# A pair mask added by GpSimd, or as the bias of ScalarE's copies of attention scores (one core)

## What is computed

```python
Q = (x @ Wq.T).reshape(b, s, h, hd)      # 16 heads of 16
K = (x @ Wk.T).reshape(b, s, h, hd)
V = (x @ Wv.T).reshape(b, s, h, hd)
scores = jnp.einsum('bshd,bstd->bsht', Q, K) / math.sqrt(hd)
attn = jax.nn.softmax(scores, axis=-1)
out = jnp.einsum('bsht,bstd->bshd', attn, V).reshape(b, s, dm)
return out @ Wfc.T
```

## Time and profile before

| | |
|---|---|
| median of three runs | 1049.65 us |
| lowest, highest | 1046.6, 1050.26 us |
| the profiled execution, first to last instruction (span) | 1045.7 us |
| mean granted PE clock over the span | 0.969 |
| PE busy | 959.2 us (92%) |
| DVE busy | 690.6 us (66%) |
| ACT busy | 496.8 us (48%) |
| POOL busy | 377.1 us (36%) |
| DMA: mean, small packets | 130 GB/s; 122142 of 133025 packets under 2 KB |

### The profile page before, as it was taken

How to read it: one execution, slowest core, us unless ns; L and a number is a source line. 1 busy time by engine, 2 the same in 40 slices (tenths; PEclk the granted TensorE clock), 3 DMA queues, 4 the chain that set the end, 5 groups by cost and what they waited for, 6 DMA issues and landing times. The chain is left out here.

```text
span 1045.7 us, 30362 instructions
## 1 busy us (share of the span) xinstructions
PE 959.2 (92%) x11177; PEld 823.6 (79%) x11178; DVE 690.6 (66%) x1747; ACT 496.8 (48%) x1343; POOL 377.1 (36%) x330
## 2 busy tenths in 40 slices
PE   6899999889999999999987999999767888999996
PEld 3466666879999999999965778888666878899995
DVE  3478877855777777777412688889985776344442
ACT  3556665404454554554446777777552440322221
POOL 0134335521223223222213455555561101455552
PEclk9999999999999999999998899999868999999998
DMA  9885581294232222221055657766421620444441
GB/s 338 216 331 122 126 269 41 97 386 115 85 102 79 87 97 85 89 92 71 8 107 92 115 124 150 154 134 128 99 68 57 266 108 22 151 134 140 134 136 35
DMA packets 133025, 135.59 MB, mean 130 GB/s; under 512 B 73884, under 2 KB 122142, under 8 KB 130740
## 3 DMA queue, kind: packets, MB, share of 16 engines
q1 hardware_dynamic: 121684, 90.80, 31.5%
q0 software_dynamic: 11232, 43.27, 13.0%
HBM read 96.21 MB, written 44.77 MB: 135 GB/s over the span
## 5 line engine op out<-in xcount | busy, mean ns | idle before, releaser
L1151 PE MATMUL psall<-rows 128*128 128x128 f32 x1872 | 224.8, 277 | 1.6 <-issue 1.1
L1151 PEld LDWEIGHTS psall<-rows 128*128 128x128 f32 x1872 | 219.6, 194 | 3.1 <-issue 1.3
L1114 POOL DMA_INDIRECT x<-ffn_rows,tok_i x78 | 82.6, 1059 | 171.8 <-DVE tok_i L999 69.9
L1165 PE MATMUL psall<-whi,rows 128*128 x624 | 141.0, 379 | 0.0
L1244 DVE COPY rows<-wlo 128x2048 f32 (+2 forms) x78 | 74.5, 955 | 95.8 <-PE psall L1151 85.2
L1165 PEld LDWEIGHTS psall<-whi,rows 128*128 128x128 f32 x624 | 115.7, 190 | 14.1
L1119 POOL DMA_INDIRECT attn_rows<-rows,tok_i x39 | 41.7, 1070 | 183.9 <-DVE rows L1276 183.9
L1504 DVE STREAM_TRANSPOSE whi<-whi 32x512 f32<-32x512 f32 x128 | 89.7, 701 | 9.1 <-POOL whi L1467 7.7
L1584 ACT ACTIVATE whi<-psall 32x512 f32<-32x512 f32 x128 | 75.3, 588 | 30.8 <-PE psall L1713 27.3
L280 PE MATMUL psall<-cst 128*128 128x128 f32 x714 | 88.4, 280 | 0.5 <-PEq L1387 0.5
L1306 ACT ACTIVATE rows<-psall,vs 128x128 f32<-128x128 f32 x312 | 85.0, 383 | 4.4 <-PE psall L1151 2.1
(11 more groups left out here) (250 smaller groups left out, 1731.3 us busy)
## 6 DMA issues: line engine op xcount, KB each, us to landing
ffn_rows<-mod_rows SPq DMA_DIRECT2D x2, 4096.0 KB
wlo<-in_W SPq DMA_DIRECT2D x2, 4096.0 KB, 17.5
whi<-in_w SPq DMA_DIRECT2D x5, 1024.0 KB
whi<-mod_rows SPq DMA_DIRECT2D x4, 1024.0 KB, 15.0
ffn_rows<-rows SPq DMA_DIRECT2D x8, 512.0 KB
ffn_rows<-x SPq DMA_DIRECT2D x8, 512.0 KB
wlo<-attn_rows SPq DMA_DIRECT2D x32, 128.0 KB, 3.4
v_turn<-wlo SPq DMA_DIRECT2D x32, 128.0 KB, 2.6
```

The source lines that it names most:

```text
L1114: eng.indirect_dma_start(xin[j % DEEP], None, src_d, bass.IndirectOffsetOnAxis(tok_i[:, j:j + 1].bitcast(U32), 0), bounds_check=T, oob_is_ ...
L1151: last = eng.matmul(b_up[t.par][f // 4][:, (f % 4) * P:(f % 4 + 1) * P], w_now[:, c, f * P:(f + 1) * P], inT[t.par][:, c * P:(c + 1) * P], ...
L1165: last = eng.matmul(b_dn[t.par][:, 0:D], hidT[t.par][:, f * P:(f + 1) * P], w_down[:, bass.ds(e, 1), f, :].rearrange("p o n -> p (o n)"), ...
```

## The change

Each quadrant's copy becomes two, by halves of the keys (16 columns of each of the 16 groups). Both are `Identity` with a per-partition bias, a 128 x 1 column of the pair mask, in place of `Copy`. `mask_other` goes, with its semaphore; `max_scores` waits for `comp` directly. The three loads of modulation rows become one of the same bytes (they lie beside each other in DRAM, in another order: GA, SB_, CB), and its users index accordingly.

```diff
@@ sync
-                        for n, j in enumerate((GA, CB, SB_)):
-                            eng.dma_start(mod3[b % 2][:, n, :], mod_d[b:b + 1, (6 + j) * D:(7 + j) * D].broadcast_to([P, D])
-                                          ).then_inc(s_m3[b % 2], 16)
+                        eng.dma_start(mod3[b % 2].rearrange("p j d -> p (j d)"), mod_d[b:b + 1, (6 + GA) * D:(7 + CB) * D].broadcast_to([P, 3 * D])
+                                      ).then_inc(s_m3[b % 2], 16)
@@ gpsimd
-                def mask_other(t):
-                    eng.wait_ge(c_["comp"], t + 1)
-                    s3 = sc[t % 3]
-                    eng.tensor_tensor(s3, s3, bc_mid(pair_mask, GR), ALU.add).then_inc(c_["msk"], 1)
-
...
-                tile_steps([(LAG_ET, normalize_exp), (LAG_X, add_attention), (LAG_MX, mask_other), (LAG_MX, sub_max)])
+                tile_steps([(LAG_ET, normalize_exp), (LAG_X, add_attention), (LAG_MX, sub_max)])
@@ vector
                 def max_scores(t):
-                    eng.wait_ge(c_["msk"], t + 1)
+                    eng.wait_ge(c_["comp"], t + 1)
...
-                        eng.wait_ge(s_m3[b % 2], 48 * (b // 2 + 1))
+                        eng.wait_ge(s_m3[b % 2], 16 * (b // 2 + 1))
...
-                    ch.do(eng.scalar_tensor_tensor(h, xr[t // TB % 3][:, t % TB, :], mean[:, 0:1], m3[:, 1, :], ALU.subtract, ALU.mult))
-                    eng.scalar_tensor_tensor(h, h, rstd, m3[:, 2, :], ALU.mult, ALU.add).then_inc(c_["h"], 1)
+                    ch.do(eng.scalar_tensor_tensor(h, xr[t // TB % 3][:, t % TB, :], mean[:, 0:1], m3[:, CB - GA, :], ALU.subtract, ALU.mult))
+                    eng.scalar_tensor_tensor(h, h, rstd, m3[:, SB_ - GA, :], ALU.mult, ALU.add).then_inc(c_["h"], 1)
@@ scalar
                         for q in quads:
                             rows_q = slice(32 * q, 32 * q + 32)
-                            last = eng.activation(sc[t % 3][rows_q], b_s[rows_q, :, 32 * q:32 * q + 32], ACT.Copy)
+                            for own in range(2):
+                                cols = slice(H * own, H * own + H)
+                                last = eng.activation(sc[t % 3][rows_q, :, cols], b_s[rows_q, :, 32 * q + H * own:32 * q + H * own + H],
+                                                      ACT.Identity, bias=pair_mask[rows_q, H * own:H * own + 1])
```

More of the change, by code:

```diff
@@ L1375, in done_by @@
             return min(max(t + lag - other - steps_ago + 1, 0), NT)
-        names = "nT hT v ve qk qke ss comp msk mx sub ex sm mul et pv oT y ya xa mv2 rs2 h tH h1T lg key"
+        names = "nT hT v ve qk qke ss comp mx sub ex sm mul et pv oT y ya xa mv2 rs2 h tH h1T lg key"
         c_ = {n: sem("c_" + n) for n in names.split()}
```

## The result

The changed kernel took 1068.97 us (median of 4 runs, 1065.29 to 1075.17), the kernel before beside it 1049.43. The ratio is 1.0197, with a 95% interval of 1.0174 to 1.0221: slower by 19.5 us by the medians and 20.7 by the ratio, where +19.8 and 1069.5 were forecast. The profiled execution took 1065.29 us, its span 1063.4. Run again later, beside other kernels, it took 1067.85, a ratio of 1.018 (1.0152 to 1.0208).

What follows compares the result with a forecast made beforehand. PE and ACT were taken to bound the kernel together in a ring. Normal steps +16.7, project steps -0.9, ACT's lateness -0.3 and drain +4.3 gave +19.8 us on 1049.65, so 1069.5, range 1056 to 1082.

Steps and rivals of the forecast that it cites:

- The ring and who pays: Normal step: closed ring from scores through ACT's copies, exps and keep_h1T to logits and scores, 6.26 us, growing to 7.33.
- The price of a step's copies: On ACT, eight biased half copies for four whole ones add 1.07 us a step, overlapping only within a quadrant.
- the bounds of 0.52 and 1.61: Added us per step for ACT's copies: +0.52 if all eight overlap, +1.61 if none does.
- The project steps: Projection starts 0.52 us later behind the copies, the 0.65 wait for DVE's gates goes: -0.13 each, -0.9 over five.
- The fill: While the pipeline fills, scores wait directly for the copies: full price of 1.07 us a step, nothing in two half-clock steps.
- The drain and what follows: Last projection pays 1.07 us directly, six normal steps before it count half: +4.3; nothing behind the last projection.
- The gain from the mask: Without POOL's mask, PE's gates wait goes: 4 x 0.65 + 0.8 in project steps, and 0.3 from ACT's lateness.
- All copies overlap: Rival: ACT's copies all overlap, 0.52 to 0.80 us a step, +6.5 to +13, 1056 to 1063 us; chance 0.18.
- No pair overlaps: Rival: none of ACT's copies overlap, 1.61 us a step, +33, 1083 us; chance 0.09.
- The clock: Rival: PE's new idleness drops its clock to half, +9 to +20 on top, 1078 to 1090 us; chance 0.08.
- The load: One load for three on SP: two DMAs less, eight times, never on the ring; zero effect.
- The bias for free: Rival: bias costs nothing and ACT's copies overlap, -0.23 us a step, -7, 1043 us; chance 0.07: 0.04 faster, 0.03 same.

Runs made afterwards that it cites:

- e5: The changed kernel with its eight half copies as Copy without a bias, the mask left out altogether: 1044.40 us, 0.9961 of the kernel before.
- e13: The kernel before with its four whole copies as Identity with a per-partition bias, the mask still on POOL: 1052.68 us, ratio 1.0037.
- e4: The changed kernel with its eight biased copies reordered, first halves of all quadrants, then second halves: 1087.95 us, 1.0352 of the kernel before.
- e2: The kernel before with POOL's mask addition left out, the maximum waiting for the four unchanged copies: 1044.22 us, ratio 0.9946.
- e12: The changed kernel itself, measured once more beside other kernels: 1067.85 us, 1.018 of the kernel before.
- e11: The changed kernel with four idle matmuls on PE ahead of weigh in normal steps: 1065.82 us, 1.0158 of the kernel before.
- e10: The kernel before with the single load and no mask in the scores; POOL's multiplied factor is 0 for the other token: 1045.55 us, ratio 0.9972.
- e6: The kernel before with POOL's mask added behind sub_max in place of ahead of the maximum: 1069.05 us, ratio 1.0187.

## Why the prediction was right, and where it was off

**The ring and who pays** stood as read. Normal steps with every stage went from 6.26 to 7.20, with PE's wait before `logits`. Over the nine of the table that is 65.4 - 56.7 = 8.7 us, and without the one long step (7.77) 0.90 each, as three steps of the kernel before were 6.38.

**The price of a step's copies** was 0.96 us (3.34 - 2.38) and not 1.07, within the bounds of 0.52 and 1.61. The mechanism held in both halves, a pointer's price and overlap only within a quadrant. The size was off since I built it up from a 128-partition row: a half without a bias is 367 ns and not the 383 of line 1570, and the pointer 91. The Trainium skill's page "ScalarE: Activation LUTs", section "What ACT_TABLE_LOAD costs", has 93 ns for a pointer and for an overlap: 91 (e5, e13) and 0.09 us (within a quadrant) agree. Its overlap does not hold between quadrants (e4), so its 0.80 a step was too low by 0.16; by its duration of 492 ns a half is 34 too long.

**The project steps** were forecast to give 0.13 each: 10.33 for 10.54 is 0.2 in three of the four. Start of the projection, gates and the end came as worked out. The fourth, 11.44 at half clock, makes the four together cost 0.3 (42.4 against 42.1).

**The fill** was forecast from its steps as if nothing else changed: about +7 of the 16.7. It gave 77.1 - 73.5 = +3.6. Four steps rose from 5.4 to 6.34 and two from 6.26 to 7.20, so they paid the price as forecast. But the step before 577.75, counted at the full price, took 7.73 us in both kernels: PE's wait before `weigh` grew from 1.00 to 1.52 us and the one before `scores` shrank from 1.34 to 0.81. And the kernel before had a step of 8.33 at half clock that the changed one did not have (6.34 in its place).

**The drain and what follows**, +4.3 forecast, gave 52.2 - 49.0 + 49.8 - 48.2 = +4.8: two projections wait 3.55 us where they waited 3.32 and 2.60. This is a net of two things, of which the forecast had one: `turn_h` waits 8.6 us for DVE where it waited 12.3, the mask's gain in the drain, and against e5, which has that gain too, the drain and the rest are 6.5 us longer.

**The gain from the mask** was put at 3.7 us and measured 5.7 (3.7 to 7.6) by itself, since the drain was left out of it. As a term to be added it was the weakest step: e13 shows that slower normal steps take away DVE's lateness at the gates without it. How much the mask's removal was worth beside eight biased copies is open; the changed kernel with POOL's mask put back was not run.

**The total** was closer than its parts, and that is partly luck. The eight biased copies were forecast at 19.8 + 3.7 = 23.5 us; between e2 and the changed kernel lie (1.0197 - 0.9946) x 1049.4 = 26 us (25 with e12's ratio), though a step's copies cost less than forecast, and the greater gain of the mask makes up for it. Which steps hold the difference is open: the two single profiles differ by only 19 us. In the main profiles the fill came out lower, and the spans differ by 17.7 us and not 19.5.

**The rivals.** All copies overlap: out by the 3.34 and by the rows of ACT under e4. No pair overlaps: out by the same, and e4 shows what it would have cost. The clock: there, in 1 or 2 steps of a run, some 2 us by e11. The load: nothing. The bias for free: out by e5 and e13.

## What to carry to other kernels

An engine at half its time is not free where it and the bound engine hand work to each other in a ring; find the ring in the timeline, and price an edit by what it adds there. Taking 1.27 us a tile off an engine with time to spare and putting 0.96 us on the ring lost 20 us. A constant that only masks was cheapest here in a factor that was multiplied with anyway (e10); moving it within its own engine's queue put it onto another ring (e6).

## What the runs showed of the hardware that was not expected

On ScalarE instructions overlapped their predecessor by 0.09 to 0.11 us only if both started at the same partition, whatever tiles they used: the same eight copies took 1.90 us per four in one order and 1.66 in the other, and the whole kernel 16 to 19 us more. A copy of 32 partitions x 256 elements is 367 ns where one of 128 x 256 is 383. One DMA of 384 KB took SP 1.2 us to issue, nearly as long as three of 128 KB (3 x 0.44).
